# GpSimd makes the low and high halves of all four groups of V from the second batch on

## The reference

```python
q = proj(Wq, bq) * scale; k = proj(Wk, bk); v = proj(Wv, bv)
q = apply_rotary(pos, q); k = apply_rotary(pos, k)
sim = jnp.einsum('bhid,bhjd->bhij', q, k)
sim = jnp.where(causal, -jnp.finfo(sim.dtype).max, sim)
attn = jax.nn.softmax(sim, axis=-1)
out = jnp.einsum('bhij,bhjd->bhid', attn, v)          # then out @ Wo + bo
x = _layernorm(x + attention); x = _layernorm(x + ffn(x))
```

## Time and profile before

| | value |
|---|---|
| median of 3 runs | 1828.95 us |
| the profiled execution: its own time, its span | 1828.78 us, 1827.0 us |
| PE busy | 1651.8 us, 90% |
| DVE busy | 1526.1 us, 84% |
| ACT busy | 1416.9 us, 78% |
| POOL busy | 1419.4 us, 78% |
| DMA, mean | 120 GB/s |
| granted TensorE clock, mean | 0.991 of full |

### The profile page before, as it was taken

One profiled execution on the slowest core, in us unless ns is written; L12 is line 12 of the kernel. 1 busy time (PEld: TensorE's weight loads), 2 busy tenths in 40 slices (PEclk: granted clock), 3 DMA queues, 4 the chain that ended last, 5 costly groups with the idle time before them and its releaser, 6 DMA issues. The chain is left out here.

```text
span 1827.0 us, 34150 instructions
## 1 busy us (share of the span) xinstructions
PE 1651.8 (90%) x10510; PEld 1007.1 (55%) x10510; DVE 1526.1 (84%) x3679; ACT 1416.9 (78%) x2570; POOL 1419.4 (78%) x1353
## 2 busy tenths in 40 slices
PE   6789898888999999998999999989999999979997
PEld 3355555554555555555555555555555555546664
DVE  7799999998888888888888888888888888865776
ACT  4688778678888888888888888888888878864664
POOL 4888888888788888788888888798888888834664
PEclk9899999999999999999999999999999999999999
DMA  3667667657766676668666666677676876560101
GB/s 113 129 131 141 120 155 145 127 103 156 140 118 123 120 137 127 123 137 152 125 127 116 127 141 116 112 151 138 123 127 125 162 135 124 107 135 1 36 24 35
DMA packets 645027, 218.43 MB, mean 120 GB/s; under 512 B 610544, under 2 KB 617200, under 8 KB 644720
## 3 DMA queue, kind: packets, MB, share of 16 engines
q1 hardware_dynamic: 620784, 174.30, 51.2%
q10 hardware_dynamic: 24064, 41.95, 8.2%
HBM read 48.40 MB, written 16.78 MB: 36 GB/s over the span
## 5 line engine op out<-in xcount | busy, mean ns | idle before, releaser
L1301 DVE SCALAR_TENSOR_TENSOR planes<-S,recip,planes 128x128 f16<-128x128 f32 (+7 forms) x512 | 417.1, 815 | 133.6 <-ACT planes L944 133.0
L944 ACT ACTIVATE planes<-S,recip 128x128 f16<-128x128 f32 (+7 forms) x512 | 378.4, 739 | 157.9 <-DVE recip L1362 139.7
L935 ACT ACTIVATE S<-p_row,neg_max 128x128 f32<-128x128 f32 (+7 forms) x512 | 381.1, 744 | 131.6 <-DVE neg_max L1291 130.8
L579 POOL TENSOR_TENSOR swap<-swap,sin_t 128x512 f32<-128x512 f32 x256 | 325.2, 1270 | 164.8 <-ACT swap L957 164.7
L1291 DVE CUSTOM_DVE_ANT_0 p_row<-S,mask_row,to_score 128x128 f32<-128x128 f32 (+7 forms) x512 | 416.8, 814 | 11.9 <-PE S L1614 9.6
L573 POOL TENSOR_TENSOR rot<-rot,swap 128x512 f32<-128x512 f32 x252 | 319.8, 1269 | 67.5 <-DVE rot L1351 63.1
L957 ACT ACTIVATE swap<-S,bqx 64x512 f32<-64x512 f32 x512 | 349.2, 682 | 22.4 <-PE S L1635 9.5
L1551 PE MATMUL O<-PT,VB 128*128 128x512 f16 (+3 forms) x1152 | 214.9, 327 | 60.2 <-issue 40.9
L1551 PE MATMUL O<-PT,VA 128*128 128x512 f16 (+3 forms) x1152 | 215.2, 328 | 56.0 <-issue 40.2
L1614 PE MATMUL S<-QKA 128*128 128x512 f16 (+4 forms) x1152 | 230.6, 327 | 5.4 <-DVE rot L1351 2.9
L1614 PE MATMUL S<-QKB 128*128 128x512 f16 (+4 forms) x1152 | 231.1, 328 | 4.4 <-POOL QKB L617 3.0
(11 more groups left out here) (227 smaller groups left out, 2727.3 us busy)
## 6 DMA issues: line engine op xcount, KB each, us to landing
PT<-planes SPq DMA_TRANSPOSE x512, 3.4
WA<-w_d ACTq DMA_DIRECT2D x24, 256.0 KB, 3.8
WB<-w_d ACTq DMA_DIRECT2D x24, 256.0 KB, 2.8
attn_d<-resid ACTq DMA_DIRECT2D x16, 256.0 KB, 3.3
x_raw<-in_x_cols SPq DMA_DIRECT2D x12, 256.0 KB, 3.7
WVA<-wv_d ACTq DMA_DIRECT2D x12, 256.0 KB, 2.6
resid<-in_x_rows ACTq DMA_DIRECT2D x12, 256.0 KB, 3.4
WVB<-wv_d ACTq DMA_DIRECT2D x12, 256.0 KB, 2.7
```

The source lines that it names most:

```text
L579: nc.gpsimd.tensor_tensor(swap[:, c, :], swap[:, c, :], sin_t[:, half], ALU.mult).then_inc(sin_done, 1)
L935: nc.scalar.activation(row_psum(n, s)[:, 0:cols], p_row[:, k % 2, 0:cols], ACT.Exp, bias=neg_max[:, s:s + 1], scale=-1.0, accum_out=row_su ...
L944: nc.scalar.activation(row_halves(n, s)[:, 0], row_psum(n, s)[:, 0:cols].rearrange("p (j q) -> p j q", q=P), ACT.Copy, scale=recip[:, s:s ...
L1301: nc.vector.scalar_tensor_tensor(halves_of[:, 1], row_psum(n, s)[:, 0:cols].rearrange("p (j q) -> p j q", q=P), recip[:, s:s + 1], halves_ ...
```

## The change

From pair 8 on GpSimd makes the halves of all four groups. v_sb becomes four tiles: three in place of the old one, and a fourth in a gap of the region behind the weights tile WA. `in_sb` holds for group 3 too, so ACT writes it to v_sb and DVE's `value_low` does nothing for these pairs. `POOL_V0` becomes `{0: 1, 4: 2, 5: 3}`: group 1 moves from step 4 to step 0 of the even head, group 2 from step 5 to step 4, and group 3 takes step 5. `v_free` and `v_whole` wait for the new counts.

```diff
-    v_sb = sb("v_sb", [P, 3, GQ])
+    v_sb = [sb(f"v_sb{i}", [P, GQ]) for i in range(3)] + [at(AT_W + 2048, "v_sb3", [P, GQ], F32)]
...
     def in_sb(pair, i):
-        return pair >= H // 2 and i < 3
+        return pair >= H // 2
     def v_free(e, k):
...
-            e.wait_ge(v_lo, k if pair < H // 2 else 2 * H + pair - H // 2 + 1)
+            e.wait_ge(v_lo, k)
     def v_whole(e, pair):
-        e.wait_ge(v_lo, 4 * pair + 4 if pair < H // 2 else 2 * H + pair - H // 2 + 1)
         if in_sb(pair, 0):
-            e.wait_ge(vp_lo, 3 * (pair - H // 2) + 3)
+            e.wait_ge(vp_lo, 4 * (pair - H // 2) + 4)
+        else:
+            e.wait_ge(v_lo, 4 * pair + 4)
...
-    POOL_V0, POOL_V1 = {4: 1, 5: 2}, {7: 0}
+    POOL_V0, POOL_V1 = {0: 1, 4: 2, 5: 3}, {7: 0}
...
-                whole, tiles = v_sb[:, i, :].rearrange("p (t c) -> p t c", t=2), slice(2 * i, 2 * i + 2)
-                k = 3 * (pair - H // 2) + i + 1
+                whole, tiles = v_sb[i][:, :].rearrange("p (t c) -> p t c", t=2), slice(2 * i, 2 * i + 2)
+                k = 4 * (pair - H // 2) + i + 1
...
-                    wait(act, vp_lo, 3 * (pair - H // 2 - 1) + i + 1)
-                    nc.scalar.activation(v_sb[:, i, :], X[:, :], ACT.Copy, scale=of_pair(v_up, pair)).then_inc(v_hi, 1)
+                    wait(act, vp_lo, 4 * (pair - H // 2 - 1) + i + 1)
+                    nc.scalar.activation(v_sb[i][:, :], X[:, :], ACT.Copy, scale=of_pair(v_up, pair)).then_inc(v_hi, 1)
```

## The result

| | before | changed |
|---|---|---|
| median | 1831.67 us (5 runs, 1828.39 to 1835.38) | 1816.46 us (5 runs, 1811.54 to 1817.86) |
| the profiled execution: its own time, its span | 1828.78, 1827.0 us | 1811.54, 1809.7 us |

The ratio is 0.9911, with a 95% interval of 0.9887 to 0.9934: faster by 0.9%. A later comparison of the same changed kernel gave 1813.71 us and 0.9923 (0.9906 to 0.9939). The prediction was 1817.2 us, with faster as the likeliest outcome.

What follows compares the result with a forecast made beforehand. TensorE was taken to wait in step 0 for VectorE, late from step 4 of the even head. 22 x 0.59 = 13.0 us gained less 1.4 at the batch turns: 1828.8 - 11.6 = 1817.2 us; 8-in-10 range 1811 to 1826.

Steps and rivals of the forecast that it cites:

- Who is late in step 0: In step 0 of both heads TensorE waits for VectorE's output_low, 0.99 us even and 1.94 odd, not for GpSimd.
- The gain of 0.59 us: Removing DVE's group 3 subtraction in step 4 brings the chain 0.59 us forward a pair; odd wait 1.94 to 1.35.
- GpSimd's cover: The added 1.81 us fit GpSimd's 3.81 us idle ahead of the even head's first sine multiply, costing nothing.
- The even heads' wait stays 0.99 us: TensorE's wait in step 0 of even heads was to remain 0.99 us.
- The turns: At heads 31 and 47 GpSimd lacks idle time; its delay hits xT in step 2, costing 0.46 and 0.94 us.
- The sum: 22 x 0.59 = 13.0 us gained, 1.4 lost at the turns: 11.6 us less, 1817.2 us.
- Rival A: VectorE held up by GpSimd's subtraction in step 0; 0.19 of 0.59 us a pair left, 1826 us; chance 0.07.
- Rival B: Gain taken back by other TensorE waits, above all DMA transposes; 1830 us, or 1824 if half gained; chance 0.16.
- Rival C: GpSimd becomes the bound, its added 1.81 us counting in every pair: 29 us more, 1858 us; chance 0.05.

Runs made afterwards that it cites:

- e2: Changed kernel with GpSimd's three groups of the even head in steps 4, 5 and 6, none in step 0: 1885.9 us (before 1826.44).
- e3: Kernel before with DVE's group 3 subtraction left out from pair 8 on, nothing added: 1816.37 us, ratio 0.9948.
- e5: Changed kernel with GpSimd's group 1 subtraction in step 0 done 3 times: 1819.55 us; 6 times: 1898.37 us (before 1831.89).
- e1: Changed kernel with TensorE's long-fulfilled wait for v_lo put back ahead of products with V from pair 8: 1819.72 us (before 1826.44).
- e6: Changed kernel with o_lo's wait written behind those for turned rows: 1814.02 us; with those moved ahead of the chunk: 1811.85 us (before 1831.89).
- second profile: The unmodified changed kernel timed and profiled again: 1813.71 us, ratio 0.9923.
- e6_early_waits: Changed kernel with the first attend's waits for turned rows moved ahead of step 0's first chunk, leaving two semaphores: 1811.85 us (before 1831.89).

## Why the prediction was right

- **Who is late in step 0.** Right. In ordinary heads PE followed DVE's output_low as that moved. The name of the even head's wait changed from GpSimd to "issue" between before and changed while the wait stayed the same kind; e2 shows what a true wait for that V subtraction looks like.
- **The gain of 0.59 us.** Right to the hundredth: 1.94 to 1.35, ACT 1.01 to 0.42, even heads 24.78 to 24.19, and by e3 due to the removal alone (the hand-over put at 0.04 us is 0.03 by its rows, 726.93 - 726.90; it changes nothing). Of the 22 ordinary even heads 18 gained 0.58 to 0.60; the sum is 12.27 us where 13.0 were forecast, mostly because head 60 gained 0.01 and head 28 0.40.
- **GpSimd's cover.** Right: the sine multiply is 0.07 us behind ACT as before, and e5 shows that a further 2.5 us is free in ordinary heads.
- **The even heads' wait stays 0.99 us.** Wrong by 0.10. I looked at DVE, ACT and GpSimd and not at PE's own waits, whose list the change shortens. It is worth 0.10 us in 13 odd heads, 1.3 us (e1). Why 0.10 isn't settled (e6).
- **The turns.** The mechanism was right, the size was off, and the first place was missed. I let GpSimd's delay act at xT, where PE waited already; it acts at the head's first scores already, where PE waits for QKB (0.47 us before, 3.11 now). Forecast were +0.46 and +0.94; measured +0.28 and +1.51, in the second profile +0.30 and +0.75. The second turn differs by how long the clock was low: until about 1209.6 in the first profile, for 3 us or so in the second. A short stretch cost nothing there, since TensorE then waits less for xT: at the first turn 1.66 us with the full clock and 0.64 with the low one, and both times the two heads took 50.7 us. Against e3, which has no added work, the turns cost 1.7 and 2.1 us (second profile 1.7 and 1.4), about the whole of the added 1.81. In these terms the forecast was 0.46 + 0.59 = 1.05 and 0.94 + 0.59 = 1.53 us, so too little at the first turn and about right at the second.
- **The sum.** 12.3 to 12.5 us in heads 16 to 62 against 11.6: 1.3 more from the start of the attend, 1.35 from head 61, about half of it because the profile of before happened to have a stretch at the lower clock there, 0.7 less from ordinary even heads, and some tenths either way at the turns and in single odd heads. That 1816.46 lies 0.7 us from 1817.2 is partly luck: the median of before was 2.7 us higher in this comparison, and the ratio of 0.9911 means 16 us, of which heads 16 to 62 explain 12 to 13; where the rest of the medians' difference lies, these profiles don't show.
- **Rival A** (VectorE held by GpSimd) is refuted: the ordinary even heads kept the whole 0.59 us and not 0.19. sum_down runs from 704.70 to 704.84, over the end of GpSimd's cast and the start of its subtraction (704.79), takes 0.14 us as before, and stands 2.33 us behind the head's first maximum in both kernels (712.03 - 709.70 and 704.70 - 702.37). It shares only some hundredths of a microsecond with the subtraction; the reciprocal behind it (704.88, 0.16 us) lies wholly inside and isn't longer than before either. The trace of before had a fuller case: its sum_down at 709.30 took 0.14 us beside GpSimd's subtraction, which ran from 708.28 to 709.43. The rule of the Trainium skill (SBUF — State Buffer, section Who interferes with whom), that a tensor_scalar can take the ports shared with GpSimd and the later of the two then blocks, does not show for this instruction of 128x1 elements.
- **Rival B** (taken back) happened nowhere in ordinary heads, apart from single ones: +0.23 in head 25, +0.31 in head 37. **Rival C** needs at least 2.5 us more work a pair, or the place of e2.

## What to carry to other kernels

Ask of a removed instruction who was late at its place, and of an added one how long its queue idled there: the same 1.8 us of work cost nothing in step 0 (changed), and with the same groups of V in steps 4, 5 and 6 TensorE's wait was 3.37 us instead of 1.35 in ordinary pairs (e2). Average shares say neither, nor does the name behind a wait: compare ends and starts. Look for the few places where the cover is missing (here the batch turns), take the added time in full there, and read the granted clock behind every wait of TensorE that became longer: where it fell in e2, it cost 1.7 us more.

## What the runs showed of the hardware

- A single wait of TensorE of 2.0 to 3.4 us, in a kernel where it is 90% busy, can be followed by 2 to 7 us at 1.2 GHz (granted clock 0.50), and need not be: the two turns of the changed kernel have the same wait of 3.11 us, and only the second one was followed by it. An odd head of e2 becomes 1.7 us longer by it, beside the wait itself; where TensorE has a later wait to fall back on, it can cost nothing (first turn, 50.72 us with the full clock and 50.74 with some 3 us of the lower one).
- A wait for a semaphore value that was reached long ago moved TensorE's start by 0.10 us (e1), though nothing is waited for. With only two waits left on the matmul (e6_early_waits) it started 0.14 to 0.15 us behind output_low, with five in the changed kernel 0.10 to 0.11.
